# Causal mask by key: a minimum on VectorE in place of mask products on TensorE

## The chip, the cores and the metric

The kernel runs on one core of a Trainium2 chip. The metric is the device time of one execution in microseconds (us). A core has TensorE (matrix products, into PSUM), VectorE, ScalarE, GpSimd and SyncE (which issues the transfers); each runs its own instruction stream in order, and they wait for one another through semaphores.

## The reference

The program is one transformer layer with modulation. Its first half is a causal attention over 8 sequences of 512 tokens, 16 heads of 8 dimensions; its second half is six layers of local attention and feed-forward. Only the causal half matters here:

```python
def _L0_attn_ref(x, Wq, Wk, Wv, Wo):
    q = (x @ Wq.T).reshape(B, S, N_HEADS, HEAD_DIM).transpose(0, 2, 1, 3)
    ...
    q, k = _apply_rope(q, k, cos, sin)
    scores = jnp.einsum('bhqd,bhkd->bhqk', q, k) / math.sqrt(HEAD_DIM)
    mask = jnp.triu(jnp.full((S, S), -jnp.inf, dtype=scores.dtype), k=1)
    scores = scores + mask[None, None]
    probs = jax.nn.softmax(scores, axis=-1)
    out = jnp.einsum('bhqk,bhkd->bhqd', probs, v)
    ...
h = _layernorm(x, axis=-1) * (1 + ca) + sa
x = x + ga * _L0_attn_ref(h, L0_attn_Wq, L0_attn_Wk, L0_attn_Wv, L0_attn_Wo)
h = _layernorm(x, axis=-1) * (1 + cb) + sb
x = x + gb * _L0_ffn_ref(h, ...)
```

## The kernel before

`part_a` is the causal half, `part_b` the six layers, `part_c` the output. The change is in `part_a` and in the table of constants.

In `part_a` the 16 heads of a sequence ("batch") go in 4 groups of 4 heads, 32 groups in all. The scores are computed twice. **By row** (`scores`, L423 and L424): queries on the partitions, so that VectorE can take the maximum of each query over its keys (the reduce at L748, negated into `negmax`). TensorE adds the causal mask with a product of the identity and `causal_mask` into the same PSUM bank (L424); three banks `tm` take turns. **By key** (`scores_by_key`, L438 and L440): keys on the partitions, with `q2`, into which the negated maxima have been added; for each head one product, and then again one product of the identity with `causal_keys` (L440) over the 128 columns of the diagonal block of each head in the bank; two banks `km` take turns. ScalarE takes the exponential into `probT` (L590), which holds three chunks of keys; a chunk is 128 keys. **`weigh`** (L454) multiplies the chunk's exponentials of the four heads with the values into `po`; a column of ones in `values` gives the sum for the division.

The order is written out by step numbers. A group has 11 row units, `ROWS` (widths 128 to 512 columns in all), and 11 key units, `KEYED`, which follow 16 steps later (`LAG`); the last units of the four chunks are at `ENDS = [4, 8, 10, 11]`, and `weigh` of a chunk follows one step behind its last exponential. In each step `s` TensorE does, in this order: fill work for other groups and batches (projections, stacking `q` and `k`, the turns at L373 into two banks `gen`), the row unit `s`, the key unit `s - LAG`, and a `weigh`, if one is due. VectorE does in each step: parts of the layer norms (L659 to L679), the rope products (L702), its two of the four `kG` copies (L711), the reciprocal (L716), the division `oN` (L723), the sum into `xtok` (L734), and last the reduce of the row unit. The normalisation of a finished batch (`h2`) and that of the next batch (`h`) meet VectorE in the last group of a batch.

```python
            def weigh(gr, k):
                b, g = divmod(gr, GROUPS)
                pe.wait_ge(exp_d, PER * gr + ENDS[k])
```

Waits that matter: the row product of unit u waits for the reduce of unit u - 3 (`max_d`), a key product for the exponential two units back (`exp_d`), `weigh` for the last exponential of its chunk, the reduce for its bank (`tm_full`), and the turn of `oT` (L373) for ScalarE's copy of `po` (L581), which waits for the last `weigh` of the group.

## Time and profile before

| | |
|---|---|
| median of 3 runs | 3744.88 us (3739.05 to 3750.31) |
| profiled execution | 3750.11 us, span 3748.0 us |
| TensorE products busy | 3597.6 us, 96% of the span |
| VectorE | 3149.5 us, 84% |
| ScalarE | 2410.4 us, 64% |
| GpSimd | 2310.4 us, 62% |
| mean granted TensorE clock | 0.984 of 2.4 GHz |

A page of the profile names engines PE (TensorE), PEld (its weight loads, which overlap products), DVE (VectorE), ACT (ScalarE), POOL (GpSimd), and lines of the kernel as L440. The causal half lies between the start and about 575 us of the span. In the profile's strips of 40 slices (3748.0 / 40 = 93.7 us each) the first six belong to it:

```profile
PE   6999995999999999999999999999999999999996
DVE  5767664998889999988899998889999988899993
ACT  4555553666667676666676766667676766676663
```

Each digit is the busy share of a slice in tenths. A product's end is modelled and overlaps the next, so what a product costs on TensorE is read from start to start.

### The profile page before, as it was taken

Reading aid. Unit: us, or ns where it says so; the run is one execution under the profiler, and the core shown is the slowest. Engines: PE = TensorE matmul, PEld = TensorE weight load, DVE = VectorE, ACT = ScalarE, POOL = GpSimd, SP = SyncE. Lnnn points to the kernel's source line nnn. Section 1 sums busy time; section 2 is a strip of 40 time slices with the busy share of each in tenths; the row PEclk is TensorE's granted clock in tenths of the full one; section 3 lists DMA queues with packets and bytes.
Section 4 is the critical chain, followed back from the end, with each engine's and each line's share of the span. In section 5 each row is a group of like instructions: output and inputs, shape, how many; then the busy total and the mean of one; then the engine's idle time right before and its main releaser. Section 6 shows DMA issues by size and latency. Waiting matters only on the chain. (4 is left out here: it accounts for less than half of the span.)

```text
span 3748.0 us, 147316 instructions
## 1 busy us (share of the span) xinstructions
PE 3597.6 (96%) x64322; PEld 2745.5 (73%) x64322; DVE 3149.5 (84%) x4991; ACT 2410.4 (64%) x3791; POOL 2310.4 (62%) x1367
## 2 busy tenths in 40 slices
PE   6999995999999999999999999999999999999996
PEld 4777773777777777777777777777777777777774
DVE  5767664998889999988899998889999988899993
ACT  4555553666667676666676766667676766676663
POOL 1110104777677777776777777777777777677771
PEclk9999997999999999999999999999999999999998
DMA  1000001222222222222122222222222112221122
GB/s 58 4 4 7 4 7 49 58 55 57 55 57 59 65 53 58 52 61 61 52 57 56 55 62 60 55 57 55 64 61 58 52 52 53 56 57 53 52 53 70
DMA packets 122997, 188.78 MB, mean 50 GB/s; under 512 B 25054, under 2 KB 44278, under 8 KB 122108
## 3 DMA queue, kind: packets, MB, share of 16 engines
q1 hardware_dynamic: 122364, 179.36, 17.7%
q8 instruction: 517, 8.47, 1.0%
q14 instruction: 116, 0.95, 0.1%
HBM read 24.08 MB, written 4.19 MB: 8 GB/s over the span
## 5 line engine op out<-in xcount | busy, mean ns | idle before, releaser
L1319 POOL TENSOR_TENSOR rc<-rc,rnorm 128x1024 f32<-128x1024 f32 x384 | 731.2, 1904 | 392.8 <-DVE rnorm L170 375.7
L1313 POOL TENSOR_TENSOR rc<-rc,rs 128x1024 f32<-128x1024 f32 x384 | 910.9, 2372 | 7.2 <-DVE rs L1378 3.6
L1354 POOL TENSOR_TENSOR prob_b<-prob_b,rinv 128x1024 f32<-128x1024 f32 x192 | 365.2, 1902 | 361.0 <-DVE rinv L1459 361.0
L1372 DVE TENSOR_TENSOR rc<-proj,rope_b 128x1024 f32<-128x1024 f32 x384 | 465.8, 1213 | 86.0 <-ACT squares L1176 85.2
L1176 ACT ACTIVATE squares<-proj 128x1024 f32<-128x1024 f32 x384 | 392.9, 1023 | 179.5 <-PE proj L928 175.9
L1019 PEld LDWEIGHTS ring<-pT,vmoved 64*64 64x64 f32 x18432 | 378.8, 135 | 133.2 <-issue 133.1
L1378 DVE TENSOR_TENSOR rs<-proj,rope_b 128x1024 f32<-128x1024 f32 x384 | 466.3, 1214 | 0.0
L965 PEld LDWEIGHTS ring<-ident,rc 128*128 128x128 f32 x3072 | 361.6, 141 | 142.6 <-issue 44.9
L1386 DVE TENSOR_REDUCE sums<-squares 128x16 f32<-128x1024 f32 x384 | 464.1, 1209 | 0.0
L965 PE MATMUL ring<-ident,rc 128*128 128x128 f32 x3072 | 428.1, 277 | 15.3 <-POOL rc L1319 11.9
L1019 PE MATMUL ring<-pT,vmoved 64*64 64x32 f32 x18432 | 402.6, 220 | 22.4 <-issue 20.8
L1019 PE MATMUL ring<-pT,vown 64*64 64x32 f32 x6144 | 377.5, 219 | 6.9 <-issue 6.9
L1167 ACT ACTIVATE qT<-ring 128x512 f32<-128x512 f32 x384 | 228.6, 595 | 203.9 <-PE ring L965 203.9
L1034 PE MATMUL proj<-oT_b,wo 128*128 128x256 f32 x1536 | 352.3, 383 | 2.5 <-issue 2.5
L926 PE MATMUL proj<-wqkv_hi,xa_hi 128*128 128x512 f32 x768 | 330.4, 430 | 24.4 <-POOL xa_lo L1295 21.1
L1167 ACT ACTIVATE vown<-ring 128x512 f32<-128x512 f32 x384 | 229.7, 598 | 177.5 <-PE ring L928 167.6
L748 DVE TENSOR_REDUCE negmax<-tm 128x1 f32<-128x384 f32 (+3 forms) x352 | 220.7, 639 | 144.4 <-PE tm L424 140.9
L1019 PEld LDWEIGHTS ring<-pT,vown 64*64 64x64 f32 x6144 | 332.6, 135 | 7.5 <-issue 7.5
L1167 ACT ACTIVATE pT<-ring 128x512 f32<-128x512 f32 x384 | 218.4, 595 | 182.9 <-PE ring L998 181.7
L985 PE MATMUL scr<-kT,qT 64*32 64x64 f32 x24576 | 332.5, 224 | 1.6 <-issue 1.4
L1167 ACT ACTIVATE kT<-ring 128x512 f32<-128x512 f32 x384 | 228.4, 595 | 161.0 <-PE ring L965 161.0
L1034 PEld LDWEIGHTS proj<-oT_b,wo 128*128 128x128 f32 x1536 | 291.5, 192 | 46.8 <-issue 4.1
(173 smaller groups left out, 7906.6 us busy)
## 6 DMA issues: line engine op xcount, KB each, us to landing
vmoved<-vown SPq DMA_DIRECT2D x576, 128.0 KB
vmoved<-vown SPq DMA_DIRECT2D x192, 192.0 KB
vmoved<-vown SPq DMA_DIRECT2D x576, 64.0 KB
wqkv_raw<-in_L_ffn_Wqkv SPq DMA_DIRECT2D x40, 192.0 KB, 3.0
wo<-in_L_ffn_Wo SPq DMA_DIRECT2D x6, 512.0 KB, 5.2
x_attended<-xtok SPq DMA_DIRECT2D x8, 256.0 KB, 2.0
xtok_c<-x_attended SPq DMA_DIRECT2D x8, 256.0 KB, 4.5
out<-xtok_c SPq DMA_DIRECT2D x8, 256.0 KB, 2.8
```

The source lines that it names most:

```text
L965: last = nc.tensor.transpose(bank[:, p * P:(p + 1) * P], rc[:, k % 2, c, o:o + P], ident[:, :])
L985: last = nc.tensor.matmul(scr[32 * w:32 * w + 32, s, p, :], qT[rows, p, 32 * w:32 * w + 32], kT[rows, p, j * P + 32 * w:j * P + 32 * w + K ...
L1019: last[i] = nc.tensor.matmul(banks[i][64 * b:64 * b + 64, p, 32 * odd:32 * odd + 32], v[64 * s:64 * s + 64, :], pT[64 * s:64 * s + 64, p, ...
L1034: last = nc.tensor.matmul(bank[:, HALVES[half]], wo[:, p, :], oT[:, p, HALVES[half]], start=(p == 0), stop=(p == PAIRS - 1))
L1167: nc.scalar.activation(dst, src, ACT.Copy).then_inc(ring_free, 1)
L1176: nc.scalar.activation(squares[:, c, :], proj[c][:, :], ACT.Square).then_inc(sq_done, 1)
L1313: nc.gpsimd.tensor_tensor(rc[:, k % 2, c, :], rc[:, k % 2, c, :], rs[:, c, :], ALU.add).then_inc(add_done, 1)
L1319: nc.gpsimd.tensor_tensor(dst, dst, rnorm[:, k % 2, c * HEADS:(c + 1) * HEADS].rearrange("p (h o) -> p h o", o=1).broadcast_to([P, HEADS, ...
L1354: nc.gpsimd.tensor_tensor(pr, pr, rinv[:, :, :].rearrange("p q (s o) -> p q s o", o=1).broadcast_to([P, PAIRS, 2, KEYS]), ALU.mult).then_i ...
L1372: nc.vector.tensor_tensor(rc[:, k % 2, c, :].rearrange("p (h d) -> p h d", h=HEADS), proj[c][:, :].rearrange("p (h d) -> p h d", h=HEADS), ...
L1378: nc.vector.tensor_tensor(rs[:, c, :].rearrange("p (h s d) -> p h s d", h=HEADS, s=2), src[:, :, ::-1, :], tab.broadcast_to([P, HEADS, 2, ...
L1386: nc.vector.tensor_reduce(sums[:, c * HEADS:(c + 1) * HEADS], squares[:, c, :].rearrange("p (h d) -> p h d", h=HEADS), AX.X, ALU.add).then ...
```

## The change

The mask product by key (L440) is gone. The key products now each open and close their own columns of the bank, and the exponential runs over unmasked scores. Behind it VectorE takes, once per chunk, the minimum of the four heads' diagonal blocks in `probT` with a table `bound`, which holds 0 where the key is after the query and 2 elsewhere. `weigh` waits for that minimum (`bounded`) and no more for the exponential. The table is a further load of 64 KB (128x128 in float32) and the mask table is one block of 128 columns smaller.

```diff
+    out["a_bound"] = np.where(np.arange(P)[None, :] < np.arange(P)[:, None], 0.0, 2.0).astype(f)
...
-    m = np.concatenate([np.where(bad, MASKED, 0.0), np.where(first, MASKED, 0.0), causal, causal.T, np.eye(P)], 1)
+    m = np.concatenate([np.where(bad, MASKED, 0.0), np.where(first, MASKED, 0.0), causal, np.eye(P)], 1)
...
+            sp.dma_start(bound[:, :], t_in["a_bound"]).then_inc(loaded, 16)
...
                 for m in range(n):
-                    nc.tensor.matmul(bank[:, m, :], kG[:, gr % K_HOMES, hh + m, k * P:(k + 1) * P], q2[:, gr % 2, k * P:TOKENS],
-                                     start=(m == 0), stop=False)
-                nc.tensor.matmul(bank[:, :, 0:P], ident_r, causal_keys.rearrange("p (o k) -> p o k", o=1).broadcast_to(
-                    [P, n, P]), start=False, stop=True).then_inc(km_full, 1)
+                    last = nc.tensor.matmul(bank[:, m, :], kG[:, gr % K_HOMES, hh + m, k * P:(k + 1) * P], q2[:, gr % 2, k * P:TOKENS],
+                                            start=True, stop=True)
+                last.then_inc(km_full, 1)
...
-                pe.wait_ge(exp_d, PER * gr + ENDS[k])
+                pe.wait_ge(bounded, 4 * gr + k + 1)
...
+                for k in range(TILES):
+                    gr = group_at(s, LAG + ENDS[k])
+                    if gr is not None:
+                        dve.wait_ge(exp_d, PER * gr + ENDS[k])
+                        diagonal = probT[:, (4 * gr + k) % 3, :, 0:P]
+                        nc.vector.tensor_tensor(diagonal, diagonal, bound[:, :].rearrange("p (o q) -> p o q", o=1).broadcast_to(
+                            [P, 4, P]), ALU.min).then_inc(bounded, 1)
```

The last loop stands at the end of each step of VectorE, behind the reduce.

TensorE, from the row unit with index 2 of a group (two heads of 256 columns) to the weigh in the next step; `gen` is fill work. Before:

```order
L423 MATMUL tm2<-kG,qG 128x512 [waits max_d]
L424 MATMUL tm2<-mask_r 128x2x128
L438 MATMUL km1<-q2,kG 128x256 [waits exp_d]
L438 MATMUL km1<-q2,kG 128x256
L440 MATMUL km1<-mask_r 128x2x128
L392 MATMUL gen0<-qk_hi,sel 128x512 [waits lo_d,g_dve]
L393 MATMUL gen0<-qk_lo,sel 128x512
L423 MATMUL tm0<-kG,qG 128x384 [waits max_d]
L424 MATMUL tm0<-mask_r 128x128
L438 MATMUL km0<-q2,kG 128x256 [waits exp_d]
L440 MATMUL km0<-mask_r 128x2x128
L454 MATMUL po<-probT,values 32x384 [waits exp_d]
```

After:

```order
L426 MATMUL tm2<-kG,qG 128x512 [waits max_d]
L427 MATMUL tm2<-mask_r 128x2x128
L441 MATMUL km1<-q2,kG 128x256 [waits exp_d]
L441 MATMUL km1<-q2,kG 128x256
L395 MATMUL gen0<-qk_hi,sel 128x512 [waits lo_d,g_dve]
L396 MATMUL gen0<-qk_lo,sel 128x512
L426 MATMUL tm0<-kG,qG 128x384 [waits max_d]
L427 MATMUL tm0<-mask_r 128x128
L441 MATMUL km0<-q2,kG 128x256 [waits exp_d]
L456 MATMUL po<-probT,values 32x384 [waits bounded]
```

The two products of `mask_r` with the key bank are gone, and the weigh waits for VectorE (`bounded`) instead of ScalarE.

VectorE, in the fourth group of the last batch, from the row unit with index 4 to that with index 9, where it also normalises the batch before (`var_t`, `xn`). Before:

```order
L748 TENSOR_REDUCE negmax<-tm1 128x1 [waits tm_full]
L723 TENSOR_TENSOR oN<-oT,gen0 128x512 [waits g_fill]
...
L748 TENSOR_REDUCE negmax<-tm2 128x1 [waits tm_full]
L711 TENSOR_SCALAR kG<-gen1,one 32x512 [waits g_fill]
L679 TENSOR_SCALAR xn<-xtok,mv,rstd 128x128 [waits g_fill,rstd_d]
...
L748 TENSOR_REDUCE negmax<-tm0 128x1 [waits tm_full]
L716 RECIPROCAL rden<-gen0 128x16 [waits wide_d,g_fill]
```

After:

```order
L750 TENSOR_REDUCE negmax<-tm1 128x1 [waits tm_full]
L758 TENSOR_TENSOR probT<-probT,bound 128x4x128 [waits exp_d]
L725 TENSOR_TENSOR oN<-oT,gen0 128x512 [waits g_fill]
...
L750 TENSOR_REDUCE negmax<-tm2 128x1 [waits tm_full]
L758 TENSOR_TENSOR probT<-probT,bound 128x4x128 [waits exp_d]
L713 TENSOR_SCALAR kG<-gen1,one 32x512 [waits g_fill]
L681 TENSOR_SCALAR xn<-xtok,mv,rstd 128x128 [waits g_fill,rstd_d]
...
L750 TENSOR_REDUCE negmax<-tm0 128x1 [waits tm_full]
L758 TENSOR_TENSOR probT<-probT,bound 128x4x128 [waits exp_d]
L718 RECIPROCAL rden<-gen0 128x16 [waits wide_d,g_fill]
```

A minimum stands behind the reduce of the units with index 2, 4, 5 and 9 of every group; what followed the reduce before now follows the minimum.

## Rows read from the trace of the kernel before

**Rows 1.** One batch period: us, then busy us (x instructions) per engine, clock

```profile
296.10:362.52 66.42, 65.72 (x450) 47.26 (x449) 46.71 (x110) 38.74 (x70) 7.51 (x9) 1.00 0.02 5
```

**Rows 2.** Waits in that period: us in total, times, longest

```profile
DVE negmax L748 <- PE tm L424: 18.2, 23, 3.2
...
PE gen L373 <- ACT oT L581: 0.5, 2, 0.2
```

**Rows 3.** Instruction groups in that period: busy us, mean ns | idle before

```profile
L440 PE MATMUL km<-mask_r 128*128 128x128 f32 x32 | 7.1, 222 | 0.0
...
L711 DVE TENSOR_SCALAR kG<-gen,one 32x512 fp32r<-32x512 f32 x8 | 6.0, 754 | 0.3
...
L440 PE MATMUL km<-mask_r 128*128 128x256 f32 x8 | 2.2, 281 | 0.0
...
L440 PE MATMUL km<-mask_r 128*128 128x512 f32 x4 | 1.8, 447 | 0.0
```

**Rows 4.** Timeline, TensorE, two places: start us, duration us, instruction

```profile
302.90 0.39 PE L393 MATMUL gen<-qk_lo,sel 128*128 128x512 f32 x1
...
303.12 0.34 PE L423 MATMUL tm<-kG,qG 128*128 128x384 f32 x1
...
306.28 0.45 PE L438 MATMUL km<-q,kG 128*128 128x512 f32 x1
...
306.57 0.22 PE L440 MATMUL km<-mask_r 128*128 128x128 f32 x1
...
306.62 0.45 PE L423 MATMUL tm<-kG,qG 128*128 128x512 f32 x1
```

**Rows 5.** Timeline, second group of a batch, units 4 to 6

```profile
319.12 0.22 PE L424 MATMUL tm<-mask_r 128*128 128x128 f32 x1
...
319.38 0.56 DVE L748 TENSOR_REDUCE negmax<-tm 128x1 f32<-128x384 f32 x1 [1.44 <-PE tm L424]
...
319.85 0.68 DVE L723 TENSOR_TENSOR oN<-oT,gen 128x512 f32<-128x512 f32 x1
...
322.38 0.43 PE L454 MATMUL po<-probT,values 128*32 128x128 f32 x8
```

**Rows 6.** Fourth group: VectorE and TensorE timeline, and its busy time

```profile
349.70:361.60 11.90, 11.53 (x91) 8.33 (x89) 11.06 (x42) 7.62 (x14) 0.00 (x0) 1.00 0.07 24
...
353.31 0.56 DVE L748 TENSOR_REDUCE negmax<-tm 128x1 f32<-128x384 f32 x1 [0.33 <-PE tm L424]
...
359.52 1.29 DVE L748 TENSOR_REDUCE negmax<-tm 128x1 f32<-128x512 f32 x2
...
361.11 1.06 PE L454 MATMUL po<-probT,values 128*32 128x512 f32 x8
...
361.61 0.69 DVE L748 TENSOR_REDUCE negmax<-tm 128x1 f32<-128x512 f32 x1
```

**Rows 7.** Timeline: ScalarE's copy of the output bank, and the turn behind it

```profile
339.54 0.60 ACT L581 ACTIVATE oT<-po 128x512 f32<-128x512 f32 x1
...
340.28 0.63 PE L373 MATMUL gen<-ident,oT 128*128 128x128 f32 x4 [0.24 <-ACT oT L581]
```

**Rows 8.** Timeline, second group of a batch, units 2 and 3

```profile
316.00 0.28 PE L424 MATMUL tm<-mask_r 128*128 128x256 f32 x1
...
316.32 0.69 DVE L748 TENSOR_REDUCE negmax<-tm 128x2 f32<-128x512 f32 x1 [0.70 <-PE tm L424]
316.36 0.28 PE L440 MATMUL km<-mask_r 128*128 128x256 f32 x1
...
317.67 0.53 PE L454 MATMUL po<-probT,values 128*32 128x384 f32 x4
```

**Rows 9.** Timeline, second group of a batch, unit 10

```profile
327.65 1.07 PE L454 MATMUL po<-probT,values 128*32 128x512 f32 x8
```

**Rows 10.** DMA issues of the page: KB each, us to landing

```profile
x_attended<-xtok SPq DMA_DIRECT2D x8, 256.0 KB, 2.0
```

**Rows 11.** Busy time per engine early in the span

```profile
20.00:60.00 40.00, 25.84 (x90) 17.12 (x89) 24.45 (x75) 9.55 (x16) 6.30 (x5) 0.87 0.02 5
```

More of the change, by code:

```diff
@@ L117, in program @@
         ident = sb("ident", [P, P])
-        masks = sb("masks", [P, 2 * KEYS + 3 * P], bf16)
+        masks = sb("masks", [P, 2 * KEYS + 2 * P], bf16)
         win_mask = [masks[:, KEYS:2 * KEYS]] + [masks[:, 0:KEYS]] * (TILES - 1)
-        ident_bf = masks[:, 2 * KEYS + 2 * P:2 * KEYS + 3 * P]
+        ident_bf = masks[:, 2 * KEYS + P:2 * KEYS + 2 * P]
         mod = sb("mod", [P, 6, BATCH])
@@ L252, in part_a @@
         one = sb("one", [P, 1])
-        mask_r = sb("mask_r", [P, 3 * P], f32r)
-        causal_mask, causal_keys, ident_r = mask_r[:, 0:P], mask_r[:, P:2 * P], mask_r[:, 2 * P:3 * P]
+        bound = sb("bound", [P, P])
+        mask_r = sb("mask_r", [P, 2 * P], f32r)
+        causal_mask, ident_r = mask_r[:, 0:P], mask_r[:, P:2 * P]
         rows = sb("rows", [DEPTH, 3 * P + 2 * FF])
@@ L295, in part_a @@
         rope_a = sem("rope_a"); hi_d = sem("hi_d"); lo_d = sem("lo_d")
-        tm_full = sem("tm_full"); max_d = sem("max_d"); km_full = sem("km_full"); exp_d = sem("exp_d")
+        tm_full = sem("tm_full"); max_d = sem("max_d"); km_full = sem("km_full"); exp_d = sem("exp_d"); bounded = sem("bounded")
         w_done = sem("w_done"); o_out = sem("o_out"); wide_d = sem("wide_d")
@@ L326, in _ @@
             sp.wait_ge(kept, 16 * BATCH)
-        NLOAD = 15 * 16
+        NLOAD = 16 * 16
         pieces = [(0, P), (P, P), (2 * P, P)] + [(3 * P + o, w) for o, w in FFC] + \
@@ L518, in _ @@
             nc.scalar.activation(sel[:, :, :], sel_raw[:, :, :], ACT.Copy).then_inc(sel_d, 1)
-            nc.scalar.activation(mask_r[:, :], masks[:, 2 * KEYS:2 * KEYS + 3 * P], ACT.Copy).then_inc(sel_d, 1)
+            nc.scalar.activation(mask_r[:, :], masks[:, 2 * KEYS:2 * KEYS + 2 * P], ACT.Copy).then_inc(sel_d, 1)
             act.wait_ge(wo_p, 1)
```

## Prediction

> **What bounds the kernel now.** I read the stretches of the windows view first. The changed code runs only in the first stage, to about 575 us of the span; there the work repeats with a period of 66.4 us for each of the 8 batches, and in one such period TensorE is busy 65.72 of 66.42 us, VectorE 46.71 [rows 1]. The waits of the same period say who follows whom: VectorE waited 18.2 us for TensorE's score products, TensorE waited for ScalarE 0.5 us and for VectorE not at all [rows 2]. So TensorE sets the pace, and VectorE has 19.7 us of room per batch, on average. The rest of the text is about where that room lies, because the change takes from the engine that is full and gives to one that is full in places.
>
> I number the 11 slots of a group as the row units are: slot 0 is the unit with four heads, slots 3 to 6 those with 384 columns. In one slot TensorE does fill work, the row products (L423, L424), the key products (L438, L440) and, in slots 10, 3, 5 and 6, a weigh (L454). VectorE's minimum stands in the slot before each of these weighs (9, 2, 4, 5), behind the reduce of that slot.
>
> **What is removed.** 11 mask products per group (8 of 128 columns, 2 of 256, 1 of 512) [rows 3], 352 in all. The step from a 128-column mask product to the next product is 0.05 us (306.57 to 306.62); that is the low price. The high price: the long product ahead of it needs 0.29 us to the next start (306.28 to 306.57), while a long product that follows a long one needs 0.22 (302.90 to 303.12), so 0.07 of weight load may go with it: 0.12 us [rows 4]. I take 0.09, since what follows is sometimes one and sometimes the other. By the durations, 222, 281 and 447 ns, the wider ones cost 0.06 and 0.22 more [rows 3]. A group saves 8 x 0.05 + 2 x 0.11 + 0.27 = 0.89 us at least, 8 x 0.12 + 2 x 0.18 + 0.34 = 1.66 at most, 1.3 if all of it counted.
>
> The pitch of a product can also be read from the Trainium skill, "TensorE: Matmul & The Clock Gate", section "Back-to-back issue gap": N/2.4 + 2.5 ns, with the weights loaded ahead. By that page a group would save 2048/2.4 + 11 x 2.5 = 0.88 us, the low end; the 0.29 against 0.22 of the trace speaks against full hiding of the loads, and the time would be about 4 us longer by it.
>
> **What is added.** 128 minimums of 128x512 in float32 on VectorE, with both inputs and the output in SBUF. Nearest rows: a two-input product of this size with one input in PSUM takes 0.68 us [rows 5]; two reduces of 512 columns in a row take 1.29, so each occupies 0.60 and its result is there 0.09 later [rows 6]. I take 0.60 of occupancy and 0.68 to the result; bounds 0.55 and 0.75. That is 16 x 0.60 = 9.6 us per batch: VectorE would be at 56.3 of some 66. A wait of TensorE for a result costs a reaction as well: ScalarE's copy ended at 340.14 and the product that waited for it began at 340.28, 0.14 us [rows 7].
>
> **Where it is hidden and where not.** The minimum makes each weigh wait for a chain on VectorE.
> Slot 2 to slot 3: the row mask product starts at 316.00, the reduce 0.32 later, the weigh at 317.67, 1.67 after [rows 8]. Now: 0.32 + 0.60 (reduce) + 0.68 + 0.14 = 1.74. TensorE would have been there at 1.67 - 2 x 0.15 = 1.37 (the two masks of 256 columns). So nothing is gained, 0.07 is lost.
> Slot 4 to slot 6: from 319.12 to the weigh at 322.38 are 3.26 [rows 5]. Now VectorE does reduce (start 0.26 later, 0.47 to the next start), minimum 0.60, the oN product 0.60, reduce 0.47, minimum 0.68, and 0.14: 3.22. TensorE would have been there at 3.26 - 0.31 - 0.18 = 2.77. Gain 0.04 of the 0.49 saved.
> Slots 7 to 1: pure TensorE, six masks at 0.09, 0.54 us. In two of the three plain groups slots 7 and 8 end in a wait for ScalarE's oT copy, which the last weigh starts [rows 2, 7]: 0.18 is lost, 0.36 left. In the second group slot 10's weigh follows the one of slot 6 by 5.27 us [rows 9], 4.91 without masks; VectorE needs from there 0.78 + 0.47 + 0.78 (the two kG copies, 754 ns each [rows 3], and a reduce), 0.72 for a rope product, three reduces 1.80, 0.68 and 0.14, less the 0.22 by which it is ahead: 5.15. It is late by 0.24.
> A plain group thus gains 0.54 - 0.24 - 0.03 = 0.27 or 0.36 - 0.03 = 0.33; 0.30 on average, 24 groups: **-7.2 us** (bounds -14.4, 0.6 each with the high mask price, and 0 with a minimum of 0.75).
>
> The fourth group of a batch is the point. There VectorE also normalises the batch before (xtok sum, statistics, two rsqrt parts, xn) and begins the statistics of the next. From 349.7 to 361.6 it is busy 11.06 of 11.90 us and idle before reduces only 0.33 us in one piece (353.31); its reduce of slot 9 begins at 361.61, later than TensorE's weigh of slot 10 at 361.11, which does not need it [rows 6]. Now that weigh needs the minimum behind it. Three minimums stand before: 361.61 - 0.33 + 3 x 0.60 = 363.08; then the reduce 0.60, the minimum 0.68, the reaction 0.14: 364.50, **3.39 us later** than 361.11. What TensorE saved before that weigh counts for nothing; behind it two masks give 0.18 back: +3.2 per such group (bounds +2.7 and +3.9). Queued behind these waits are slots 0 and 1, so the loss is not absorbed. Six batches of row work have it in full: **+19.2 us**. The first has no batch before it (the 1.8 us of next statistics alone: +1.3), the last no next one (+1.4): **+2.7 us**.
> Behind the last row unit VectorE is empty and slots are short, so each weigh waits exponential, minimum, weigh: **+1.0** (0 to 2). The start waits for 64 KB more of loads; 256 KB land in 2.0 us [rows 10], so 0.5 at most: **+0.3**. ScalarE, GpSimd and the second stage get nothing: the exponential already ends a slot before its minimum, and the buffer of three chunks is freed in time by weighs that are late by under a slot.
> Sum: -7.2 + 19.2 + 2.7 + 1.0 + 0.3 = **+16.0 us**. Against the profiled execution (3750.11 us) that is 3766.1; that execution lies 5.2 above the median of the runs, 3744.88, which has the same work, so the forecast is 3744.9 + 16 = **3761 us**.
>
> **Rivals.**
> Full gain: VectorE keeps up in every slot and TensorE stays the bound. For it: 19.7 us idle against 9.6 added [rows 1]. Against: the 0.33 us of idle in the fourth group. 32 groups x 1.3 = -41: 3704; with the low price -28: 3717. Chance 0.08. It is faster where I forecast slower.
> Half of it: the plain groups gain more than I allow (a faster reaction, a cheaper minimum, the full mask price, about 0.85 each), the fourth group loses 2.7: 24 x -0.85 + 16 + 4 = 0: 3745. This decides by whether the chains of slots 3 and 6 end before TensorE comes. Chance 0.20, within 11 us of the time before in half of its cases, a quarter on either side.
> Clock: TensorE at half clock after the new gaps. In the fourth group it would have about 10.7 us of work in 15.3, 70%; between 20 and 60 us it was busy 25.84 of 40 and the granted clock was 0.87 of 2.4 GHz [rows 11]. At 0.87 the work takes 1.6 us more in six groups: +10 more, 3771. Chance 0.07. The same page of the Trainium skill, section "Part 1: The HAM clock gate", has the clock fall after idleness; the batch periods here, at a granted clock of 1.00, show no gap that would try it.
> The change not doing what it says: if the minimum cost a slot of its own on the path (0.68 + 0.14 for each of 128), +105: 3850. Chance 0.01, since the order puts it behind work that TensorE does not await.
>
> **How the numbers follow.** Forecast case 0.64, its own range +3 to +28: 3748 to 3773 (low: -14.4 + 16.2 + 1.6; high: 0 + 23.4 + 2.7 + 2). With the half rival down to 3736 and the clock rival up to 3778 the range holds 8 in 10; the full gain and the far ends stay out. A measurement tells 0.3%, 11.2 us, from no change. Slower by more: 0.47 of the forecast case's 0.64, 0.07, 0.01 and 0.05 of the half rival: 0.60. Faster by more: 0.08 and 0.05: 0.13. The rest, 0.27, is between.
>
> **What the profile after would show.** The period of a batch at about 68.7 us in place of 66.4, with plain groups 0.3 shorter and the fourth 3.2 longer; 128 minimums at 0.68 us; 1.74 us from the row mask product of slot 2 to the weigh of slot 3, and 3.22 from slot 4 to slot 6; TensorE waiting at L456 of the new file for VectorE, longest in slot 10 of the fourth group; VectorE busy near 56 us per batch. The forecast is wrong if the fourth group's slot 10 weigh comes less than 2 us late, or if a weigh in a plain group doesn't wait at all.

## The result and the profile after

The changed kernel takes 3789.32 us (median of 5 runs, 3786.3 to 3797.55) against 3744.88: 1.0117 times as long, with a 95% interval of 1.0102 to 1.0133, or **+44.4 us**. The sign was forecast; the size was not: +16 us was predicted, and the time lies above the range's upper end of 3778. The profiled execution took 3787.08 us, 36.97 more than that of before.

From the page of after, the busy time of each engine with its share of the span:

```profile
span 3784.9 us, 146741 instructions
...
PE 3586.6 (95%) x63970; PEld 2714.2 (72%) x63970; DVE 3217.5 (85%) x5119; ACT 2408.6 (64%) x3791; POOL 2309.7 (61%) x1367
```

TensorE has 352 products fewer and only 11 us less of busy time; VectorE has 128 instructions and 68 us more.

Below, the "first stage" is the causal half and the "second stage" the six layers behind it. The first stage can be cut at GpSimd's copy of `rden` in the first group of each batch. The stretches between these copies, of before: the first batch, one of the five equal ones, the last, and the tail up to the first GpSimd instruction of the second stage (columns: stretch, its length, then busy us and instructions of TensorE, its loads, VectorE, ScalarE, GpSimd, then the granted clock):

```profile
81.20:142.94 61.74, 61.18 (x430) 44.67 (x427) 42.71 (x87) 37.45 (x68) 7.50 (x9) 1.00 0.01 1
209.35:275.76 66.41, 65.70 (x449) 47.26 (x448) 46.71 (x109) 38.73 (x70) 7.50 (x9) 1.00 0.02 5
...
474.98:536.93 61.95, 60.83 (x429) 44.40 (x428) 40.50 (x83) 36.38 (x66) 2.46 (x5) 1.00 0.02 6
536.93:590.40 53.47, 42.28 (x270) 26.33 (x268) 19.19 (x64) 19.98 (x37) 2.87 (x9) 0.90 0.03 10
```

The same stretches of after, all of them:

```profile
81.60:147.86 66.26, 61.05 (x390) 41.65 (x391) 51.21 (x103) 36.53 (x67) 7.49 (x8) 0.97 0.00 1
147.86:216.82 68.96, 62.65 (x405) 42.39 (x404) 55.35 (x125) 38.56 (x70) 7.50 (x8) 1.00 0.01 5
216.82:287.35 70.53, 64.19 (x405) 43.70 (x404) 55.45 (x125) 38.55 (x70) 7.50 (x8) 0.98 0.01 5
287.35:358.97 71.62, 65.30 (x405) 43.94 (x404) 55.46 (x125) 38.57 (x70) 7.50 (x8) 0.95 0.01 5
358.97:430.63 71.66, 65.31 (x405) 43.97 (x404) 55.47 (x125) 38.55 (x70) 7.50 (x8) 0.95 0.01 5
430.63:502.26 71.63, 65.34 (x405) 43.99 (x404) 55.45 (x125) 38.55 (x70) 7.49 (x8) 0.95 0.01 5
502.26:567.11 64.85, 57.64 (x385) 39.49 (x384) 49.28 (x99) 36.23 (x66) 2.45 (x4) 1.00 0.01 5
567.11:621.70 54.59, 39.04 (x240) 22.80 (x238) 26.06 (x75) 20.14 (x37) 2.83 (x8) 0.90 0.03 10
```

Read the length together with the clock. The one equal batch at clock 1.00 takes 68.96 us: 2.55 more than before. The same 405 recorded products take 70.53 at clock 0.98 and 71.6 at 0.95. So two things are added, one in every batch, one in some. The start of the second stage moves from 590.4 to 621.7 us, **+31.3**: 0.4 at the start, 4.5 in the first batch, 22.4 in the five, 2.9 in the last, 1.1 in the tail. What is left of the profiled executions' 36.97 is in the second stage.

The waits of the stretch 147.86 to 216.82 of after (the batch at clock 1.00), who waited for whom, in us, times and longest:

```profile
DVE negmax L750 <- PE tm L427: 12.2, 12, 1.9
...
PE po L456 <- DVE probT L758: 5.0, 10, 1.9
```

The second line did not exist before [rows 2]: TensorE waits at 10 of the 16 weighs of a batch for VectorE's minimum. VectorE in turn waits 12.2 us for TensorE where it waited 18.2.

### The profile page after: what moved, and what is told of

Read it like the earlier page. It is cut to its first block and busy times, and to the rows that moved or that the text cites. A ratio compares the mean times of both kernels' runs of the same rounds, so it can differ in the third digit from the quotient of the medians.

```text
span 3784.9 us, 146741 instructions
## 1 busy us (share of the span) xinstructions
PE 3586.6 (95%) x63970; PEld 2714.2 (72%) x63970; DVE 3217.5 (85%) x5119; ACT 2408.6 (64%) x3791; POOL 2309.7 (61%) x1367
## 5 line engine op out<-in xcount | busy, mean ns | idle before, releaser
L974 PE MATMUL ring<-ident,rc 128*128 128x128 f32 x3072 | 429.8, 278 | 13.6 <-POOL rc L1328 11.5
L592 ACT ACTIVATE probT<-km 128x512 f32<-128x512 f32 (+1 forms) x352 | 193.7, 559 | 233.6 <-PE km L441 231.2
```

The source lines that it names most:

```text
L974: last = nc.tensor.transpose(bank[:, p * P:(p + 1) * P], rc[:, k % 2, c, o:o + P], ident[:, :])
```

## Experiments

The two theories of the first stage: **chain** (weighs wait for the order of VectorE's work, worst in slot 10 of the fourth row group) and **clock** (the waits let TensorE's clock drop). For the second stage: nothing in it was changed, so either its later start in time matters, or where it stands in TensorE's instruction stream. Behind each run, "first stage" is the shift of the first GpSimd instruction of the second stage (`mean_w`) against 590.4 us in before, and a batch is a stretch of one period. Times are medians; a ratio, with its 95% interval, is against before run on the same chip, which took 3745.66 us (no minimum, beside, fourth group keeps its mask, GpSimd), 3746.29 (the three later weighs, filler) or 3754.36 (the rest).

**No minimum.** The mask product and the minimum are both left out; the output lacks the mask by key.

```diff
-                pe.wait_ge(bounded, 4 * gr + k + 1)
+                pe.wait_ge(exp_d, PER * gr + ENDS[k])
...
-                        nc.vector.tensor_tensor(diagonal, diagonal, bound[:, :].rearrange("p (o q) -> p o q", o=1).broadcast_to(
-                            [P, 4, P]), ALU.min).then_inc(bounded, 1)
```

> The changed kernel without the minimum: no mask product by key and no clearing of the masked exponentials, so the output leaves out the causal mask of the weights. It prices the 352 mask products alone. Theory A (the minimum costs by what waits for it, the mask products are worth 0.9 to 1.7 us per group): first stage 28 to 50 us shorter than before, the time 3695 to 3720 us. Rival B (the mask products lie beside other work): within 8 us of before. For the second stage: if its slow stretches are placed by the position in the instruction streams, they start at the same sequences as in the changed kernel, three sequences earlier than before; if by the time at which the stage starts, they move.

3723.97 us, 0.9943 [0.9924, 0.9962]; first stage -27.9 us. One batch of it:

```profile
328.08:391.25 63.17, 61.78 (x406) 42.00 (x405) 46.51 (x109) 38.43 (x70) 7.52 (x9) 1.00 0.02 5
```

63.17 against 66.42: four groups save 3.25, **0.81 us for a group's 11 mask products**, under my low bound of 0.89. The time lies 4 us above the range that I had put for it. The step from product to product of [rows 4] was read as 0.05 to 0.12; it was worth less, since some of it goes into waits for ScalarE's copy of `oT` (0.8 us in this batch, where it was 0.5).

**Minimum beside the path.** The same 128 minimums, from another source into a tile of their own; the weigh waits for the exponential. The mask by key is again missing from the output.

```diff
+        beside = sb("beside", [P, 4, P])
...
-                pe.wait_ge(bounded, 4 * gr + k + 1)
+                pe.wait_ge(exp_d, PER * gr + ENDS[k])
...
-                        dve.wait_ge(exp_d, PER * gr + ENDS[k])
+                        need(dve, bounded, 4 * gr + k)
-                        diagonal = probT[:, (4 * gr + k) % 3, :, 0:P]
-                        nc.vector.tensor_tensor(diagonal, diagonal, bound[:, :].rearrange("p (o q) -> p o q", o=1).broadcast_to(
+                        source = rope[:, :, 0:P]
+                        nc.vector.tensor_tensor(beside[:, :, :], source, bound[:, :].rearrange("p (o q) -> p o q", o=1).broadcast_to(
```

> The changed kernel with the same 128 minimums at the same places on VectorE, but reading the rope table and writing a tile of their own, and with the weigh waiting for the exponential as before: the output leaves out the causal mask of the weights. It keeps VectorE's load and takes the wait away. Theory A (the wait of the weigh costs): first stage 8 to 30 us shorter than before, the fourth group still about 1 us late by the kG copies and reduces, time 3720 to 3740. Rival B (VectorE's load alone costs): first stage as long as in the changed kernel, 31 us longer than before, time 3775 to 3790.

3746.16 us, 1.0002 [0.999, 1.0015]; first stage -5.7. A batch at full clock:

```profile
207.38:273.18 65.80, 62.05 (x405) 41.97 (x404) 55.02 (x125) 38.55 (x70) 7.53 (x9) 1.00 0.02 5
```

And, from the waits of the stretch 360.96 to 426.77, TensorE's longest for VectorE:

```profile
PE tm L427 <- DVE negmax L751: 1.0, 1, 1.0
```

This splits the cost, between batches at full clock. From 63.17 to 65.80 the minimum costs **2.6 us a batch by occupancy alone**: no one waits for it, but in the fourth group what stands behind it on VectorE comes late, and TensorE waits for that (1.0 us for a reduce, 0.8 for a copy of `kG`). From 65.80 to 68.96, **3.2 us**, is what the weigh's wait for it adds. Even with no one waiting for the minimum, a batch is only 0.6 us shorter than before. Neither theory had that: the first stage was expected to be 8 to 30 us shorter than before, or 31 longer. Three of its batches take 66.5 to 66.9 us: in each the wait of 1.0 us was followed, within 3 us, by 3.4 us at 1.2 GHz. In the other batches the same wait left the clock at 2.4.

**Fourth group keeps its mask.** The 4 of 16 chunks whose minimum falls into VectorE's crowded fourth row group (the key work of groups 1 and 2 is done there) keep the mask product and have no minimum.

```diff
+def masked(gr, k):
+    return (gr % 4, k) in ((1, 1), (1, 2), (1, 3), (2, 0))
...
+                if masked(gr, k):
+                    pe.wait_ge(exp_d, PER * gr + ENDS[k])
+                else:
+                    pe.wait_ge(bounded, bounds_before(gr, k) + 1)
...
-                    if gr is not None:
+                    if gr is not None and not masked(gr, k):
```

> The change in three of four groups: the four chunks whose minimum would fall into the fourth group of a batch on VectorE keep their mask products and have no minimum. Theory A (the fourth group carries the loss, the others gain 0.2 us each, and the clock fell because of the fourth group's gap): no half-clock stretch in the steady batches, batch period 65.6 to 66.4 us against 66.4 before and 69.0 to 71.6 changed, time 3735 to 3748. Rival (the loss is spread over the groups): three quarters of it stay, period 68.3 to 70.3, time 3768 to 3778.

3743.67 us, 0.9996 [0.9982, 1.0009]; first stage -1.1. A batch of it:

```profile
310.38:376.18 65.80, 63.40 (x419) 43.56 (x422) 52.81 (x122) 38.51 (x71) 7.51 (x8) 1.00 0.02 5
```

Its wait for minimums:

```profile
PE po L476 <- DVE probT L778: 1.9, 7, 0.4
```

Without four of the 16 minimums, and with their 11 mask products back, the period is 3.16 us under the 68.96 of after. The long wait is gone too (0.4 at most, from 1.9), and so is every drop of the clock within the batches. With 12 minimums left the period is 0.6 us under before.

**GpSimd instead.** GpSimd clears the masked exponentials with a product with a table of 0 and 1; VectorE has no minimum.

```diff
+                        pool.wait_ge(exp_d, PER * gr + ENDS[k])
+                        diagonal = probT[:, (4 * gr + k) % 3, :, 0:P]
+                        nc.gpsimd.tensor_tensor(diagonal, diagonal, bound[:, :].rearrange("p (o q) -> p o q", o=1).broadcast_to(
+                            [P, 4, P]), ALU.mult).then_inc(bounded, 1)
```

> The changed kernel with the clearing done by GpSimd, as a product with a table of 0 and 1 in place of the minimum with 0 and 2 (it holds as long as no masked exponential overflows). GpSimd is 10 percent busy in this stage and takes about 1.28 us for a product of 128x512. Theory A (what costs is the chain behind VectorE's reduce and its full fourth group): GpSimd starts at the end of the exponential, and the weigh a step later finds it done or nearly, first stage 20 to 45 us shorter than before, time 3700 to 3725. Rival (1.3 us from exponential to weigh is too long at slots 5 and 6, or GpSimd slows VectorE by the memory they share): no gain, 3740 to 3770.

3759.12 us, 1.0029 [1.0015, 1.0043]; first stage +7.7. A batch:

```profile
364.48:432.19 67.71, 63.76 (x412) 42.28 (x404) 49.62 (x110) 38.83 (x71) 27.65 (x24) 0.98 0.01 5
```

TensorE's wait for GpSimd in it:

```profile
PE po L456 <- POOL probT L626: 1.6, 3, 1.0
```

And from the timeline of the fourth group in the same batch, a product of GpSimd and an instruction of VectorE beside it:

```profile
420.86 1.28 POOL L626 TENSOR_TENSOR probT<-probT,bound 128x512 f32<-128x512 f32 x1 [1.78 <-ACT probT L592]
...
421.01 1.14 DVE L155 TENSOR_TENSOR var_t<-rstd 128x4 f32<-128x4 f32 x1
```

The weighs wait 1.6 us in place of 5.0, yet the period is 67.7, part of it clock (0.98); at full clock it is 66.2. VectorE, which has the work of the first experiment, is busy 49.62 us where it was 46.51 there. Nearly all of the 3.1 us are in a few instructions of the normalisation, all with inputs and output in SBUF: the one shown took 0.19 us on the mean in the first experiment and here ends with GpSimd's product, and those that write `xn` take 471 ns on the mean in place of 342. The reduces, which read PSUM, are as long as they were. So the work moved to an idle engine costs the engine next to it, here in the fourth group, where that engine is full.

**Weigh a step later**, in three forms: after, the kernel that keeps the fourth group's masks, and the one with GpSimd, each with this one line more:

```diff
-WEIGH_AFTER = 1
+WEIGH_AFTER = 2
```

> The changed kernel with every weigh two steps behind its last exponential in place of one, so that a minimum has a step more. Theory A (the chains into the weighs of the plain groups cost 3.2 us per batch, VectorE's load in the fourth group 2.6): the first cost goes, the second stays, batch period 65.8 to 66.9 us against 69.0 to 71.6 in the changed kernel, first stage 0 to 10 us longer or shorter than before, time 3740 to 3757. Rival (VectorE stays late by more than a step, so the weigh waits as long one step later): period above 68, time above 3770.

3775.07 us, 1.0077 [1.0062, 1.0092]; first stage +17.9, as the rival had it.

> Both cures together: the four chunks whose minimum would fall into the fourth group of a batch keep their mask products, and every weigh stands two steps behind its exponential. Theory A: 12 of 16 chunks keep TensorE's saving (0.81 us per group by the kernel without the minimum, so 2.4 us per batch), nothing waits: batch period 63.8 to 64.6 us, first stage 15 to 22 us shorter than before, second stage up to 6 longer, time 3723 to 3740. Rival (the waits have another source than the chains): period as with the mask kept alone, 65.8, time 3740 to 3746.

3750.64 us, 1.0013 [0.9999, 1.0026]; first stage +6.2. A batch takes 67.1 us, more than both cases had.

> The kernel with GpSimd's product in place of the minimum, and every weigh two steps behind its exponential. In the one-step form VectorE was busy 49.6 us per batch against 46.5 without the minimum, so GpSimd slows it by 3 us, and the weighs waited for GpSimd for 1.6 us on TensorE and 3 us in its weight loads. Theory A (the waits are what costs): period 63.5 to 65.5 us, first stage 8 to 24 us shorter than before, time 3722 to 3745. Rival (what costs is that GpSimd slows VectorE, above all in the fourth group): period above 66.5, time above 3748.

3768.51 us, 1.0055 [1.0034, 1.0076]; first stage +15.2. The later weigh did not bring what I looked for in any of them, and in two it cost: against the same kernel with the weigh one step behind, the first stage grew by 7.3 (fourth mask kept) and 7.5 (GpSimd). A batch of the first form, and below it two of its waits:

```profile
320.75:389.81 69.06, 63.15 (x405) 42.01 (x405) 55.91 (x126) 37.70 (x71) 7.51 (x8) 1.00 0.01 5
```

```profile
PE gen L376 <- ACT oT L583: 2.2, 3, 1.1
PE po L456 <- DVE probT L758: 1.3, 2, 1.1
```

The wait for the minimum falls from 5.0 to 1.3 us, and the turn, which needs ScalarE's copy of a `po` that the last weigh fills, now waits 2.2 where it waited nothing. At full clock the period is what it was, 69.06 against 68.96. That the first stage is still 13.4 us shorter than in after comes mostly from fewer drops of the clock (one, of 3.4 us, where after has five batches with one).

**Filler.** After, with a key product repeated 10 times in slot 10 of the fourth row group, where TensorE waits longest; the output is unchanged.

```diff
+                extra = 10 if gr % 4 == 2 and i == 5 else 0
+                for _ in range(extra):
+                    nc.tensor.matmul(bank[:, 0, :], kG[:, gr % K_HOMES, hh, k * P:(k + 1) * P], q2[:, gr % 2, k * P:TOKENS],
+                                     start=True, stop=True)
```

> The changed kernel, in which TensorE repeats the key product of slot 10 in the fourth group of a batch ten times ahead of the real one, about 1.8 us of products that it does while it would wait 1.9 us for VectorE's minimum. Theory A (that gap is what lets the granted clock fall to 1.2 GHz behind it, at a cost of 1.6 or 2.7 us per batch): the granted clock stays at 1.00 through the stage, every batch period is 69.0 us, time 8 to 12 us below the changed kernel, 3776 to 3782. Rival (the clock falls for another reason, or filling delays the next work): periods stay above 70, time 3787 or more.

3768.19 us, 1.0057 [1.004, 1.0074], first stage +23.4: with 80 products more the kernel is 22 us above before, where after is 44. Two stretches of it, which answer to the first and fourth of after (the five equal ones take 68.94 to 68.98):

```profile
83.30:147.98 64.68, 61.27 (x400) 42.15 (x400) 51.06 (x103) 36.52 (x67) 7.49 (x9) 1.00 0.00 1
...
285.89:354.87 68.98, 64.40 (x415) 44.07 (x414) 55.34 (x125) 38.56 (x70) 7.51 (x9) 1.00 0.01 5
```

With the gap filled the clock holds in every batch and each takes 68.97 us. Against that, after loses 1.6, 1.6, 2.7, 2.7 and 2.7 us in its first, third, fourth, fifth and sixth stretch: **11.2 us are clock**. (The first stage as a whole fell by 7.9 only, since the filler kernel started 1.7 us later and its last stretches are 1.6 longer.) The rest of its gain, some 15 us, is in the second stage, which this edit does not touch; that is more than I had expected for the whole (8 to 12 us), and the table of positions below bears on it.

**Minimum first.** After, with the minimum ahead of the reduce of its step, not behind it:

```diff
+                        nc.vector.tensor_tensor(diagonal, diagonal, bound[:, :].rearrange("p (o q) -> p o q", o=1).broadcast_to(
+                            [P, 4, P]), ALU.min).then_inc(bounded, 1)
                 if 0 <= s < NU:
...
                                             negate=True).then_inc(max_d, 1)
...
-                        nc.vector.tensor_tensor(diagonal, diagonal, bound[:, :].rearrange("p (o q) -> p o q", o=1).broadcast_to(
-                            [P, 4, P]), ALU.min).then_inc(bounded, 1)
```

> The changed kernel with each minimum ahead of its step's reduce on VectorE in place of behind it: the exponential it needs ended a step earlier, so the weigh no longer waits for row product, reduce and minimum in a chain. Theory A (the chain costs 3.2 us of the 69.0 us period, VectorE's load in the fourth group the rest): period 65.8 to 67.0 us as in the kernel whose minimum nobody awaits, first stage 0 to 8 us shorter than before, time 3738 to 3752. Rival (the reduces, now later, stop the row products instead): period 68.5 or more, time above 3765.

3769.81 us against 3754.36 for before on the same chip, 1.0042 [1.0029, 1.0055]; first stage +9.8. The waits for the minimum in the batch 210.19 to 280.59 are down to three:

```profile
PE po L456 <- DVE probT L748: 2.4, 3, 1.3
```

The reduce alone was some 0.6 us of each chain. At full clock a batch takes 67.5 us, 1.5 less than in after. But the weigh of slot 10 in the fourth group still waits, since what stands ahead of its minimum there is the normalisation, two copies of `kG` and the reduces of earlier steps. The clock still drops in three batches (70.4 us the longest), and the time came out as the rival had it, for another reason: the row products were not what waited longest.

**Both.** Minimum first, and the fourth group keeps its masks.

> Minimum ahead of the reduce, and the four chunks whose minimum would fall into the fourth group of a batch keep their mask products. Theory A: nothing waits in the plain groups and nothing is added in the fourth; 12 of 16 chunks keep TensorE's 0.81 us per group: period 63.9 to 64.8 us, first stage 13 to 20 us shorter than before, second stage as before, time 3725 to 3735. Rival (another chain takes the place): period 65.8 as with the mask kept alone, time 3741 to 3746.

3743.34 us against 3754.36 on the same chip: **0.996 [0.9948, 0.9973]**, faster than before and, each against before on its own chip, than after; first stage -12.4, just short of the 13 to 20 expected. A batch of it:

```profile
205.96:270.87 64.91, 63.32 (x416) 43.40 (x416) 54.35 (x121) 38.46 (x70) 7.50 (x9) 1.00 0.02 5
```

A batch is 1.5 us shorter than before, and TensorE's wait for minimums is down to one of 0.3 us in it. The plain groups' chains were worth 65.80 - 64.91 = 0.9 us a batch; 75% of the masks are gone, and 1.5 us of the 2.4 that 0.81 us a group would bring are kept.

**The second stage: time or position.** One edit delays the second stage of before by 29.5 us with five memsets on VectorE between the stages, and leaves TensorE's instructions alone. The other adds 64 instructions to TensorE (16 tiny products, float32, which come to 32 products and 32 loads) at the end of the first stage of before; its second piece below starts 0.1 us later than that of before, so it delays nothing.

```diff
+            for i in range(5):
+                need(dve, spare, i)
+                nc.vector.memset(probT[:, :, :, :], 0.0).then_inc(spare, 1)
```

> The kernel before with five memsets of 128x6144 on VectorE between the last work of the first stage and the second, about 32 us in which nothing else runs, and no instruction more on TensorE. If the changed kernel's second stage is longer because it starts later: its slow stretches move and the time is 3745 + 32 + 6 or more. If what places them is the position in TensorE's instruction stream: they start at sequences 3, 14, 24 and 35 as before, and the time is 3745 + 32 = 3777, within 4.

3786.04 against 3754.36, +31.7 us, 1.0082 [1.0069, 1.0095], for a first stage of +29.5.

```diff
+            for _ in range(16):
+                nc.tensor.matmul(km[0][0:32, 0:8], ident[:, 0:32], ident[:, 0:8], start=True, stop=True)
```

> The kernel before with 16 tiny float32 products (32 weight loads and 32 products, 64 instructions) on TensorE at the end of the first stage, under 3 us of work. The change takes 704 instructions from TensorE's stream, which is 64 more than a multiple of 256; if code arrives in pieces of 256 instructions (16 KB each by the bytes and packets of the instruction queue) and a piece that arrives at the wrong moment of a sequence delays it, 64 more instructions put the second stage in the changed kernel's place: slow stretches from sequences 1, 11, 22, 33 and 43 in place of 3, 14, 24 and 35, time 2 to 3 us for the products and 4 to 7 us for the stretches above before, 3751 to 3756. If the position does not matter: stretches as before, time 3747.

3760.79 against 3754.36, **+6.4 us**, 1.0017 [1.0007, 1.0027], for a first stage of -0.1 (590.3). That figure also says where this chip is slower than the one of the first comparison (3754.36 against 3744.88): behind the first stage. The second stage is 48 nearly equal pieces of 62.7 us, each from one copy into `hid` on VectorE to the next; every ten or eleven pieces, some three to five in a row are slow, most of them 64 to 69 us. Where the first such stretch begins is the mark. Pieces 2, 4 and 5 of before:

```profile
805.90:868.70 62.80, 62.79 (x1266) 48.58 (x1265) 57.75 (x86) 43.55 (x68) 46.34 (x26) 1.00 0.21 56
...
931.40:996.50 65.10, 62.66 (x1195) 48.62 (x1194) 55.50 (x81) 41.53 (x66) 45.23 (x26) 0.97 0.20 54
996.50:1063.80 67.30, 65.44 (x1335) 50.42 (x1334) 59.33 (x92) 45.57 (x70) 47.43 (x27) 1.00 0.20 52
```

Pieces 2 and 5 of the delay:

```profile
834.80:897.70 62.90, 62.89 (x1265) 48.59 (x1265) 57.62 (x86) 43.50 (x68) 46.37 (x26) 1.00 0.21 56
...
1024.90:1092.70 67.80, 65.13 (x1334) 50.34 (x1332) 58.80 (x90) 45.21 (x69) 47.55 (x27) 1.00 0.20 52
```

The same two with the added instructions:

```profile
806.00:871.90 65.90, 63.04 (x1213) 48.90 (x1197) 54.96 (x82) 41.48 (x66) 44.80 (x26) 0.97 0.20 53
...
1008.60:1071.30 62.70, 62.70 (x1266) 48.47 (x1265) 57.66 (x85) 43.44 (x68) 46.31 (x26) 1.00 0.21 56
```

And the second of after, whose fifth takes 62.70 us too:

```profile
838.10:903.90 65.80, 63.19 (x1281) 48.90 (x1266) 57.28 (x85) 43.47 (x68) 46.32 (x26) 1.00 0.20 53
```

Delayed by 29.5 us, the slow stretch begins at the fourth piece (64.50 us) and has the fifth in it, as in before. With 64 instructions more and no delay it has the second, third and fourth (65.90, 69.20, 67.50), and the fifth is back at 62.70, as in after. So position in TensorE's instruction stream places it, not time. After has 704 instructions fewer there (352 products and 352 loads). How much one packet of instructions holds can be read from the queues of before:

```profile
q8 instruction: 517, 8.47, 1.0%
q14 instruction: 116, 0.95, 0.1%
```

Together they bring 9.42 MB for the 147316 instructions of the page, 64 bytes each, and a packet of the first is 8.47 MB / 517 = 16.4 KB: 256 instructions. 704 fewer and 64 more differ by 768, three whole packets, and leave the second stage at the same place in its packet. The kernels with 528 and 544 fewer stand 16 and 32 instructions short of a whole number of packets, and in all four the first piece of 64 us or more is the fifth, one later than before. So the place goes by packets of 256 in all the kernels here.

The Trainium skill ("Runtime: NRT & Kernel Launch", section "Instruction fetch mechanics") has each engine's instructions come in blocks of 16 KiB, 256 instructions, with the crossing of a block mostly hidden. The size of the packets agrees. Most pieces do run at 62.7 us, but here the position in a block is worth some 6 us, as follows; that it is the fetching that costs them, no run shows.

The eight kernels at the one position have a slow stretch more, the fifth, at the end of the stage. Pieces 44 to 46 of before, and the same with the added instructions:

```profile
3478.60:3664.10 185.50, 184.56 (x3716) 142.38 (x3713) 167.90 (x254) 125.36 (x192) 132.52 (x73) 1.00 0.20 54
```

```profile
3488.60:3681.70 193.10, 186.78 (x3734) 144.62 (x3735) 167.45 (x255) 125.53 (x192) 132.58 (x73) 1.00 0.20 52
```

In the profiles of all eight these three pieces take 190.6 to 195.4 us, in the six others, before among them, 185.3 to 185.8.

Over the whole stage single profiled executions scatter by more than that, so the effect on time is read from the medians: median against before of the same chip, less the shift of the first stage in the profile:

| TensorE instructions, against before | kernels | median shift less first-stage shift, us |
|---|---|---|
| -704 | after; no minimum; beside; GpSimd; weigh later; GpSimd and later; minimum first | +13.1; +6.2; +6.2; +5.8; +10.9; +7.0; +5.7 |
| +64 | added instructions | +6.5 |
| 0 | delay | +2.2 |
| -528 | fourth keeps mask; and later; and minimum first | -0.9; -1.9; +1.4 |
| -544 | filler | -1.5 |

The eight kernels at the one position lie at +5.7 or more, the five at others at +2.2 or less. A single row would not carry this (the interval of the added instructions, 1.0007 to 1.0027, is 2.6 to 10.1 us), but no kernel is out of line. What the fetched packets collide with was not tried.

## Why the prediction was off

Two steps failed: the clock, which the sum put at nothing and the runs at 11.2 us, and "the second stage gets nothing", where the medians show 13.1. With the clock alone the kernel would have come to 3744.9 + 31.3 = 3776 us, inside the range; the second stage took it out.

**What bounds the kernel** was read rightly: TensorE sets the pace, VectorE's room is uneven, and the fourth group is where it ends.

**The price of the minimum** (0.60 of occupancy, 0.68 to the result). The group of minimums in the batch 168.90 to 237.87 of after:

```profile
L758 DVE TENSOR_TENSOR probT<-probT,bound 128x512 f32<-128x512 f32 x16 | 11.0, 688 | 0.0
```

688 ns on the mean. The Trainium skill ("VectorE: DVE Perf Modes", section "The TRN2 errata — SBUF-src ops pay a fixed extra latency per instruction") gives (N + 151) / 0.96 for a two-input add in float32, 691 ns at 512: the trace agrees for the minimum.

**The chains of the plain groups** came as put. Timeline of after, slots 2 to 6 (start us, duration us, instruction; in brackets the idle time before it and what ended it):

```profile
314.82 0.29 PE L427 MATMUL tm<-mask_r 128*128 128x256 f32 x1
...
315.75 0.68 DVE L758 TENSOR_TENSOR probT<-probT,bound 128x512 f32<-128x512 f32 x1
...
316.58 0.85 PE L456 MATMUL po<-probT,values 128*32 128x384 f32 x8 [0.27 <-DVE probT L758]
...
318.04 0.23 PE L427 MATMUL tm<-mask_r 128*128 128x128 f32 x1
...
321.26 0.42 PE L456 MATMUL po<-probT,values 128*32 128x128 f32 x8 [0.24 <-DVE probT L758]
```

314.82 to 316.58 is 1.76 us (1.74 predicted, 1.67 before [rows 8]), and 318.04 to 321.26 is 3.22 (3.22 predicted, 3.26 before [rows 5]). The minimum ends at 316.43 and the weigh starts at 316.58: a reaction of 0.15, where 0.14 was put from [rows 7].

**The fourth group** too. From the row mask product of slot 2 to the weigh of slot 10, in a batch at full clock:

```profile
152.22 0.28 PE L427 MATMUL tm<-mask_r 128*128 128x256 f32 x1
...
168.81 1.07 PE L456 MATMUL po<-probT,values 128*32 128x512 f32 x8 [1.91 <-DVE probT L758]
```

16.59 us; in before the same stretch (347.95 to the weigh at 361.11 of [rows 6]) is 13.16. That is 3.43 later, 3.39 predicted. The period of a batch at full clock grew by 2.55, where the sum had 2.3: a period of 68.96 for the 68.7 foretold.

**Where it failed.** The sum, term by term, in us:

| term | put at | came |
|---|---|---|
| full batches (plain and fourth groups), without clock | 2.3 each, 11.5 in five | 2.55 each, 12.75 |
| first batch | 0.4 (-0.9 + 1.3) | 2.9 |
| the rest: sixth full and last fourth group, tail, load | 4.1 | 4.4 |
| clock | 0 in the sum; +10 at a chance of 0.07 | 11.2 |
| second stage | "gets nothing" | +6 by position; another 7 by the medians |
| sum | 16.0 | 44.4 |

The first three lines, 20.1 us in all, were right but for 4 us; 2.5 of these are the first batch, taken for nearly free since no finished batch is there to be normalised. The stretch shows otherwise: 66.26 us, of which 1.6 are clock, against 61.74. Its weigh of slot 10 waits as long as those of the later batches:

```profile
98.30 1.26 PE L456 MATMUL po<-probT,values 128*32 128x512 f32 x8 [1.92 <-DVE probT L758]
```

VectorE has no idle time between 88.87 us and the end of that minimum: two earlier minimums, the division, two copies of `kG`, reduces and the next batch's statistics fill it. The wait does not need a finished batch.

The **clock** rival had nearly the right price in all, 10 for 11.2 us, and a wrong chance, 0.07. The price was in part luck: it was 1.6 us in each of six groups, and came as 1.6 in two batches, 2.7 in three and nothing in one. The chance rested on the batches of before, whose clock is 1.00 and which show no gap. TensorE's longest wait in them is 0.4 us, so they could not speak against a fall behind 1.9 us, and the one row of a partly idle engine, 25.84 of 40 us at 0.87 [rows 11], spoke for it. Two short stretches of after:

```profile
229.00:239.00 10.00, 6.17 (x40) 3.69 (x40) 9.64 (x31) 5.34 (x10) 0.61 (x1) 1.00 0.00 1
239.00:242.40 3.40, 3.40 (x11) 2.92 (x11) 1.86 (x6) 0.98 (x2) 0.00 (x0) 0.50 0.00 0
```

And from its timeline, 70 us later:

```profile
308.31 1.94 PE L456 MATMUL po<-probT,values 128*32 128x512 f32 x8 [1.92 <-DVE probT L758]
```

TensorE was busy 6.17 of 10.00 us, and the next 3.4 us ran at half clock (1.2 GHz, 0.50 in the clock column). The same weigh one batch on, right behind the same gap, took 1.94 us in place of 1.07. The same gap two batches back, at 168.81, left the clock alone, though TensorE was busy 6.20 us of the ten before it. A wait that long is not needed either: behind waits of 1.0 us (minimum beside) and, with GpSimd, behind several of 0.4 to 0.8 us in a row the clock fell in some batches too. The filler shows that the gap in slot 10 is what it takes in after; what decides between one batch and the next is open.

**"The second stage gets nothing"** is the step that failed outright. It holds for the stage's work and not for its speed. A reason was given for buffers and exponentials only; that a change of TensorE's instruction count in the first stage moves everything behind it in the instruction stream was not thought of. Of the 13.1 us, about 6 are common to all kernels at that position. The other 7 have no cause that a run shows: the profiled execution of after has a second stage longer by 5.7 us only (that of before lies 5.2 above its median, that of after 2.2 below), the interval of the ratio leaves 7 to 18.5 us for it, and "weigh later" has 10.9 as well. It may be the scatter of a median of five, or something that the later minimums leave behind; that stays open.

The **mask price** was too high a saving, and so put the forecast too low as well. Taken as 1.3 us per group (0.89 to 1.66), it was 0.81. It did little harm, because the chains take most of the saving anyway; with 0.81 the full gain had no ground: with neither mask nor minimum the kernel took 3724 us, and the full gain was put at 3704 to 3717.

The range was too narrow because clock and second stage were treated as other cases and not as terms that may come on top of the forecast.

## What to carry to other kernels

Before work is moved to an engine with idle time on average, look at the step where that engine is fullest and ask who will wait for it there; where it is full, leave the work where it was (the version that did so in 4 of 16 chunks, and put the rest ahead of other work, is 0.4% faster than before, while the full move is 1.2% slower). A new gap on TensorE can cost twice, once as the wait and again as clock: if the profile of before has no gap of that kind, it has no evidence against it, and the clock belongs into the range of the forecast. In a kernel that one engine bounds, count a few us for the mere shift of the instructions behind an edit, and take no effect of that size for the edit's own until a pad has been tried.

## What the hardware showed that I had not expected

- The same wait of 1.9 us in slot 10 left the clock at 2.4 GHz in one batch, and came with 1.2 GHz for about 3.4 us in two and 6.8 us in three, at 1.6 and 2.7 us of time each. Eighty useless products in that gap kept it at 2.4 GHz and saved 11 us.
- 64 instructions added to TensorE's stream, with no delay of the second stage, made the kernel 6.4 us slower. They moved the first slow pieces of the second stage from the fourth and fifth to the second to fourth and added a slow stretch at its end (193.1 us for three pieces of 185.5); a delay of 29.5 us did not.
- 16 products on GpSimd in a batch, of 1.28 us each, lengthened VectorE's busy time from 46.51 to 49.62 us with the same work. Only instructions from SBUF to SBUF grew: one of 128x4 elements, 0.19 us on the mean alone, took 1.14 us and ended with the GpSimd product beside it.
